# One-hot rows of a group by one VectorE comparison, and source lines of seven groups by one

## The chip, the cores and the metric

The program runs on one core of one Trainium2 chip. The metric is device time in microseconds (us) for one execution of the whole program, as the median of several runs. The engines are TensorE (PE, with its weight loads as PEld), VectorE (DVE), ScalarE (ACT), GpSimd (POOL) and SyncE (SP, which here only issues DMAs).

## What is computed

Four graph layers run one after the other on 3125 nodes of 32 features with 100000 edges sorted by destination. After each layer comes `x = layernorm(x + layer(x))`.

```
def _L0_gnn_ref(h, ...):                       # relation layer with attention
    x = h[src]; y = h[dst]
    msg = jnp.einsum('eb,ebo->eo', w_comp[etype], jnp.einsum('ei,bio->ebo', x, weight))
    a = tanh(relu(sum((x @ A1_w.T + A1_b) * (y @ A2_w.T + A2_b + rel_emb[etype]), -1) / scale))
    nei = segment_sum(a[:, None] * msg, dst)
    curr = h[src[last_e]] @ self_loop_weight   # last edge of each destination
    return relu(where(in_deg > 0, nei + curr, 0))
def _L1_gnn_ref(x, ...):  return segment_sum(x[src], dst)
def _L2_gnn_ref(h, ...):  softmax over a destination's edges, weighted sum of h[src]
def _L3_gnn_ref(feat, ...): ten steps of normalized propagation over the same edges
```

## The kernel before

There are two stages. The **sweep** (`run_sweep` on every engine) goes over the edges once. It computes layer 0 and, beside it, builds an adjacency matrix of edge counts, one byte for each pair of source and destination, in `adj_bytes`. The **dense** stage (`run_dense`) computes layers 1 to 3 as matrix products with that matrix. A general path for unsorted inputs exists and is not run.

The edges are cut into 196 groups of 512 (four slots of 128). For a group g the engines do this:

- **POOL** gathers the source rows of x by indirect DMA, one instruction for each 128 edges (line 587, 674 of them, into the ring `xp` of 21 groups). Of every seven groups one is *picked*: its rows come from TensorE products with one-hot matrices and POOL gathers nothing for it. POOL waits only until a ring place is free (`mixed_used`, g - 20), and starts with 21 groups ahead before the sweep.
- **SP** loads, for each *chunk* of seven groups, the relation and destination numbers of 3584 edges into 106 partitions (`load_lines`, two halves), and for every group the rows of the destination table; it also stores each group's result rows, one at a time (line 500).
- **DVE**, in this order for a group: `score_edges` (L1285, L1286), `make_pairs(g + 1)` (L1269, L1271), `make_line(g + 4)` (L1254), on some groups `make_dst_hot` (L1258), `make_pick_hots` (L1312: four compares on the second group of a chunk, three on the third) or `read_picked` (L1319, L1324), then `make_mixed` (L1293, L1296, L1300).
- **ACT**: the tanh of the scores (L1015), `make_rows(g + 2)` (L971, L975), the copy of the counts from PSUM (L980, L984), of the sums (L994), and the move of a page of counts into `adj_bytes` (L1008).
- **PE**: `fetch(g + 1)` (L696: destination and relation values by one-hot products with the compared lines), `count(g + 1)` (L709: adjacency counts, `row_hot` against `pair_hot`), on some groups `pick_tile` (L762), `sum_mixed(g)` (L728).

`row_hot` holds for each of the 512 edges a one-hot row of 128 over the low seven bits of its source; `pair_hot` a one-hot row over destination offset and the high bits. `row_no` and `pair_no` count columns; `row_f` and `pair_of` hold the wanted column of each edge, one value for each partition and slot. Before the change slot 0 of `row_hot` is made by ACT (`make_rows`: the square of the distance, then relu of one minus it), slots 1 to 3 by DVE, and `count` waits for both. `lines` holds two chunks; each group's 512 columns are compared in place with the partition's number (L1254), four groups ahead of use. The sweep's end passes through the last gather, the last group, its stores by SP, and a reload of the stored rows, for which the dense stage waits.

Of the kernel before, what the change touches and what calls it, by code (L numbers as in the profile page):

```python
# [21 lines left out]
P = 128  # L22
# [18 lines left out]
SLOTS = 4  # L41
GROUPS = -(-TILES // SLOTS)
# [18 lines left out]
LINE_AHEAD = 4  # L61
# [10 lines left out]
ROWS_BY_SCALAR = 1  # L72
# [88 lines left out]
def gnn(nc, x_pad, edges, src_cols, pick_rows, dst_cols, next_cols, bases, dst_rows_in, rel_rows_in, a1_rows, a2_rows, rel_emb_cols,  # L161
         weight, w_comp, w_comp_t, self_loop, a1_t, a2_t, rel_emb, attn_w, out):
    ctx = ExitStack()
    with ctx:
# [3 lines left out]
        def sem(name):  # L168
# [70 lines left out]
        row_f, pair_of, dst_off, last_off_1 = [stay.cut(GROUPS * SLOTS).rearrange("p (g k) -> p g k", k=SLOTS)  # L239
                                            for _ in range(4)]  # L240
# [142 lines left out]
        row_distances, row_hot_ready = sem("row_distances"), sem("row_hot_ready")  # L383
# [274 lines left out]
        def _(pe):  # L658
# [24 lines left out]
            def run_sweep():  # L683
                pe.wait_ge(sweep_cleared, 1)

                def fetch(g):
                    c = g // LINE
                    pe.wait_ge(lines_ready, g + 1)
                    pe.wait_ge(side_in[g % SIDES], 16 * (g // SIDES + 1))
                    if g >= 2:  # L690
                        pe.wait_ge(mixed_ready, g - 1)
                    for k in range(SLOTS):
                        at = FETCHED + g % 2 * BANK + k * REL_COLS
                        e = g % LINE * WINDOW + k * P
                        for j in range(3):
                            mm = nc.tensor.matmul(ps[:, at:at + REL_COLS], lines[:, c % 2, e:e + P], side[:, g % SIDES, j, :],  # L696
                                                  start=(j == 0), stop=(j == 2))
                    mm.then_inc(fetched, 1)

                def count(g):  # L700
                    pe.wait_ge(pairs_ready, g + 1)
                    pe.wait_ge(row_hot_ready, g + 1)
# [238 lines left out]
        def _(act):  # L941
# [21 lines left out]
            def run_sweep():  # L963
                act.wait_ge(sweep_cleared, 1)

                def make_rows(g):
                    h = g % 2
                    if g >= 2:
                        act.wait_ge(pairs_used, g - 1)
                    for k in range(ROWS_BY_SCALAR):  # L970
                        last = a.activation(row_hot[:, h, k, :], row_no[:], ACT.Square, bias=row_f[:, g, k:k + 1], scale=-1.0)  # L971
                    last.then_inc(row_distances, 1)
                    act.wait_ge(row_distances, g + 1)
                    hot_rows = row_hot[:, h, 0:ROWS_BY_SCALAR].rearrange("p k v -> p (k v)")
                    a.activation(hot_rows, hot_rows, ACT.Relu, bias=1.0, scale=-1.0).then_inc(row_hot_ready, 1)  # L975

# [34 lines left out]
                make_rows(0)  # L1011
                make_rows(1)
                for g in range(GROUPS):
# [3 lines left out]
                    if g + 2 < GROUPS:  # L1017
                        make_rows(g + 2)
# [100 lines left out]
        def _(dve):  # L1119
# [77 lines left out]
            link(v.tensor_copy(row_f, row_of))  # L1197
# [43 lines left out]
            def run_sweep():  # L1241
# [7 lines left out]
                def make_line(g):  # L1249
                    c = g // LINE  # L1250
                    if g % LINE == 0:
                        dve.wait_ge(line_in[c % 2], 32 * (c // 2 + 1))
                    own = lines[:, c % 2, g % LINE * WINDOW:(g % LINE + 1) * WINDOW]
                    v.tensor_scalar(own, own, side_no[0:SIDE, 1:2], None, ALU.is_equal).then_inc(lines_ready, 1)  # L1254
# [8 lines left out]
                def make_pairs(g):  # L1263
                    h = g % 2
                    if g >= 2:
                        dve.wait_ge(pairs_used, g - 1)
                    for k in range(SLOTS):
                        if k >= ROWS_BY_SCALAR:
                            v.tensor_scalar(row_hot[:, h, k, :], row_no[:], row_f[:, g, k:k + 1], None, ALU.is_equal)  # L1269
# [56 lines left out]

                for g in range(LINE_AHEAD):
                    make_line(g)
                make_dst_hot(0)
                make_pairs(0)  # L1330
                for g in range(GROUPS):
# [3 lines left out]
                    if g + LINE_AHEAD < GROUPS:  # L1335
                        make_line(g + LINE_AHEAD)
# [506 lines left out]
```

## Time and profile before

| | |
|---|---|
| median of 3 runs | 1260.72 us (1260.57 to 1262.55) |
| the profiled execution | 1265.35 us, its span 1263.6 us |
| sweep, about 57 to 930 us of the span | 196 groups |
| dense stage, from 934 us | TensorE at a granted clock of 0.95 |
| busy over the span | PE 77%, DVE 81%, ACT 50%, POOL 55% |
| from 190 to 890 us | DVE 85 to 90%, PE 74 to 81%, ACT 58 to 62%, POOL 77% |

An instruction's busy time is from its start to its end; instructions of one engine that do not wait for each other overlap by a part, so the distance of two starts is shorter than a duration. POOL's 77% is of the gather instructions alone: the time between them is told as idle, with its reason.

### The profile page before, as it was taken

The numbers are of one execution on the slowest core, as the hardware profiler recorded it, in microseconds if no ns is written. First come the engines' busy times: TensorE is split into PE (matmuls) and PEld (weight loads), VectorE is DVE, ScalarE is ACT, GpSimd is POOL, SyncE is SP. The second block draws the span as 40 slices with busy tenths as digits, with TensorE's granted clock in tenths as the row PEclk, the third lists the DMA queues.
The fourth block names the chain that finished last, engine by engine and source line by source line (L and its number), as shares of the span: only waits on it lengthen the run. The fifth ranks groups of instructions, "written<-read, shape, count | busy, mean of one in ns | idle before, by whom it ended". The sixth has DMA issues, their size and how long they took to land.

```text
span 1263.6 us, 58393 instructions
## 1 busy us (share of the span) xinstructions
PE 977.7 (77%) x23808; PEld 898.6 (71%) x23808; DVE 1020.9 (81%) x3443; ACT 638.0 (50%) x1731; POOL 698.4 (55%) x686
## 2 busy tenths in 40 slices
PE   2368788788788787787788677767827995999996
PEld 2357677677677676676677566666726995999996
DVE  8679999889888988898889888888844997655556
ACT  1146666656565555565566555555688980000000
POOL 5777777777777777777777777777600000000000
PEclk9557777777777767767777777767758997999998
DMA  4522222122222221122122212221100000000001
GB/s 108 73 46 56 51 46 46 46 48 48 47 46 46 46 45 45 45 46 45 45 46 46 44 46 45 45 45 41 18 14 3 3 4 3 4 4 4 4 4 18
DMA packets 55896, 46.32 MB, mean 37 GB/s; under 512 B 37442, under 2 KB 51837, under 8 KB 55624
## 3 DMA queue, kind: packets, MB, share of 16 engines
q1 hardware_dynamic: 34056, 31.45, 8.9%
q0 software_dynamic: 21568, 11.09, 6.9%
q8 instruction: 190, 3.11, 1.1%
q14 instruction: 82, 0.67, 0.2%
HBM read 40.19 MB, written 2.28 MB: 34 GB/s over the span
## 4 chain that ended last, share of the span: by engine, by line
PE 25%; DMA 21%; DVE 17%; issue 14%; SPq 11%; POOL 10%; ACT 1%; DVEq 0%; POOLq 0%; ACTq 0%
PE ps L820 12%; POOL arena L587 10%; DMA arena<-line_table 10%; DMA agg_table<-arena 8%; PE ps L762 3%; SPq L519 3%; SPq L496 3%; PE ps L728 3%; DMA arena<-x_pad,arena 3%; DVE arena L1271 2%; SPq L520 2%; SPq L500 2%; DVE arena L1465 2%; DVE arena L1269 1%; PE ps L709 1%
## 5 line engine op out<-in xcount | busy, mean ns | idle before, releaser
L587 POOL DMA_INDIRECT arena<-x_pad,arena x674 | 696.5, 1033 | 205.8 <-issue 200.3
L728 PE MATMUL ps<-arena 128*32 128x44 f32 (+3 forms) x7832 | 204.9, 234 | 152.5 <-DVE arena L1300 152.1
L728 PEld LDWEIGHTS ps<-arena 128*32 128x32 f32 x7832 | 152.4, 133 | 192.7 <-DVE arena L1300 167.3
L1271 DVE TENSOR_SCALAR arena<-pair_no,arena 128x275 bf16<-128x275 f16 (+2 forms) x784 | 239.2, 308 | 0.0
L820 PE MATMUL ps<-arena,adj_words 128*128 128x64 f16 (+1 forms) x6250 | 195.7, 193 | 24.5 <-DVEq L1415 21.8
L820 PEld LDWEIGHTS ps<-arena,adj_words 128*128 128x128 fp8e4 x6250 | 193.5, 98 | 26.6 <-DVEq L1415 22.6
L1300 DVE TENSOR_TENSOR arena<-ps,arena 128x768 f32<-128x768 f32 x196 | 188.0, 959 | 6.7
L709 PE MATMUL ps<-arena 128*128 128x175 bf16 (+3 forms) x1567 | 164.0, 261 | 31.3 <-DVE arena L1271 30.4
L762 PE MATMUL ps<-aggT 128*128 128x128 bf16 x2268 | 175.3, 244 | 0.0
L1015 ACT ACTIVATE arena<-arena 128x4 f32<-128x4 f32 x196 | 40.2, 205 | 266.7 <-DVE arena L1286 255.9
L762 PEld LDWEIGHTS ps<-aggT 128*128 128x128 bf16 x2268 | 159.2, 112 | 0.0
L1269 DVE TENSOR_SCALAR arena<-row_no,arena 128x128 bf16<-128x128 bf16 x588 | 159.1, 272 | 0.0
L1008 ACT ACTIVATE adj_words<-arena 128x500 uint8 x196 | 126.2, 644 | 49.4 <-issue 38.6
L709 PEld LDWEIGHTS ps<-arena 128*128 128x128 bf16 x1567 | 121.0, 115 | 37.1 <-DVE arena L1271 36.1
L696 PE MATMUL ps<-arena 106*128 106x49 bf16 x2352 | 112.1, 201 | 7.7 <-DMA arena<-dst_parts 7.7
L984 ACT ACTIVATE arena<-ps 128x500 fp8e4<-128x500 f32 x196 | 113.2, 577 | 0.0
L980 ACT ACTIVATE arena<-ps 128x500 bf16<-128x500 f32 x196 | 111.6, 569 | 0.0
L1089 ACT ACTIVATE stat<-stat,eps 128x4 f32<-128x4 f32 (+3 forms) x9 | 2.7, 299 | 214.7 <-DVEq L1376 214.7
L1254 DVE TENSOR_SCALAR arena<-arena,side_no 106x512 bf16<-106x512 bf16 x196 | 67.2, 344 | 48.4 <-DMA arena<-line_table 48.4
L696 PEld LDWEIGHTS ps<-arena 106*128 106x128 bf16 x2352 | 93.5, 108 | 10.6 <-issue 7.9
L1285 DVE TENSOR_TENSOR arena<-ps,arena 128x132 f32<-128x132 f32 x196 | 56.3, 287 | 35.8 <-DMA arena<-x_pad,arena 24.8
L971 ACT ACTIVATE arena<-row_no,arena 128x128 bf16<-128x128 bf16 x196 | 75.7, 386 | 10.6 <-DVEq L1247 10.5
(213 smaller groups left out, 1261.7 us busy)
## 6 DMA issues: line engine op xcount, KB each, us to landing
arena<-line_table SPq DMA_DIRECT2D x28, 602.0 KB
arena<-x_pad,arena POOLq DMA_INDIRECT x674, 3.3
arena<-line_table SPq DMA_DIRECT2D x28, 140.0 KB
arena<-pick_table SPq DMA_DIRECT2D x27, 128.0 KB
arena<-dst_parts SPq DMA_DIRECT2D x196, 5.7 KB
agg_table<-arena SPq DMA_DIRECT2D x196, 2.5 KB
dst_parts<-aggT SPq DMA_DIRECT2D x1, 735.0 KB, 14.7
x<-x_pad SPq DMA_DIRECT2D x1, 400.0 KB
```

The lines of the kernel that those rows point to most:

```text
L587: pool.indirect_dma_start(to, None, table, bass.IndirectOffsetOnAxis(ap=index, axis=0)).then_inc(done, 16)
L696: mm = nc.tensor.matmul(ps[:, at:at + REL_COLS], lines[:, c % 2, e:e + P], side[:, g % SIDES, j, :], start=(j == 0), stop=(j == 2))
L709: mm = nc.tensor.matmul(ps[:, at + d0 * BLOCKS:at + d1 * BLOCKS], row_hot[:, h, k, :], pair_hot[:, h, k, (d0 - first) * BLOCKS:(d1 - first ...
L728: return nc.tensor.matmul(to.rearrange("p (d m) -> p d m", m=MIX_COLS)[:, :, 0:m1 - m0], rows_of_slot, factors[:, :, m0:m1], start=False, ...
L762: mm = nc.tensor.matmul(ps[:, at:at + PICK_WIDE * FEAT], pick_hot[:, j, k * P:(k + 1) * P], x_parts[:, t, j * PICK_WIDE:(j + 1) * PICK_WID ...
L820: mm = nc.tensor.matmul(ps[:, at:at + cols], adj[:, b, j * P:(j + 1) * P], parts[:, half, b, 0:cols], start=(b == 0), stop=(b == BLOCKS - 1))
L980: a.activation(squares, ps[:, at:at + PAIRS], ACT.Square, accum_out=square_sums[:, g:g + 1])\
L984: a.activation(pages[:, g % PAGES], ps[:, at:at + PAIRS].rearrange("p (d b) -> p b d", d=PAGE), ACT.Copy, saturate=False).then_inc(counts_ ...
L1008: a.activation(adj_bytes[:, :, bass.ds(base, PAGE)], page_bytes[:, g % PAGES], ACT.Copy)\
L1269: v.tensor_scalar(row_hot[:, h, k, :], row_no[:], row_f[:, g, k:k + 1], None, ALU.is_equal)
L1271: last = v.tensor_scalar(pair_hot[:, h, k, 0:n], pair_no[:, 0:n], pair_of[:, g, k:k + 1], None, ALU.is_equal)
L1300: v.tensor_tensor(mixed[:, g % 2, :, :, 0:BASES], fetched_of(g)[:, :, SCORED:REL_COLS].unsqueeze(2).to_broadcast(n), weighted.unsqueeze(3) ...
```

## The change

Three things are changed, all in the sweep.

1. **Rows.** A new table `row_twice` replaces `row_f`: the wanted column of each edge as a two-byte number, written twice side by side (one copy of 1568 elements before the sweep, where 784 were copied). `make_pairs` then makes all four slots of `row_hot` with one tensor_tensor compare of 512 elements for each partition, and after it the four compares of `pair_hot`, now back to back. `make_rows` and its two ACT instructions for each group are gone, with their semaphores, and `count` waits for DVE alone.
2. **Lines.** One tensor_scalar compare covers the 3584 columns of a chunk, where there were seven of 512.
3. **Their place.** The first chunk is compared before the loop, and chunk c + 1 in group 5 of chunk c (`LINES_AT`), after the pair compares. TensorE's `fetch` waits once for each chunk.

```
@@ -69,7 +68,7 @@
-ROWS_BY_SCALAR = 1
+LINES_AT = LINE - 2
@@ -236,8 +235,8 @@
-        row_f, pair_of, dst_off, last_off_1 = [stay.cut(GROUPS * SLOTS)...
+        pair_of, dst_off, last_off_1 = [stay.cut(GROUPS * SLOTS)... for _ in range(3)]
+        row_twice = stay.cut(2 * GROUPS * SLOTS, BF16).rearrange("p (g k i) -> p g k i", k=SLOTS, i=2)
@@ -685,7 +683,8 @@ (fetch)
-                    pe.wait_ge(lines_ready, g + 1)
+                    if g % LINE == 0:
+                        pe.wait_ge(lines_ready, c + 1)
@@ -699,7 +698,6 @@ (count)
-                    pe.wait_ge(row_hot_ready, g + 1)
@@ -1008,14 +995,10 @@ (ACT)
-                    if g + 2 < GROUPS:
-                        make_rows(g + 2)
@@ -1194,7 +1177,7 @@
-            link(v.tensor_copy(row_f, row_of))
+            link(v.tensor_copy(row_twice, row_of.unsqueeze(3).to_broadcast([P, GROUPS, SLOTS, 2])))
@@ -1246,11 +1229,9 @@
-                def make_line(g):
...
-                    own = lines[:, c % 2, g % LINE * WINDOW:(g % LINE + 1) * WINDOW]
+                def make_lines(c):
+                    dve.wait_ge(line_in[c % 2], 32 * (c // 2 + 1))
+                    own = lines[:, c % 2, :]
                     v.tensor_scalar(own, own, side_no[0:SIDE, 1:2], None, ALU.is_equal).then_inc(lines_ready, 1)
@@ -1264,9 +1245,11 @@ (make_pairs)
+                    n = [P, SLOTS, P // 2, 2]
+                    v.tensor_tensor(row_hot[:, h].rearrange("p k (v i) -> p k v i", i=2),
+                                    row_no[:].rearrange("p (v i) -> p v i", i=2).unsqueeze(1).to_broadcast(n),
+                                    row_twice[:, g].unsqueeze(2).to_broadcast(n), ALU.is_equal)
                     for k in range(SLOTS):
-                        if k >= ROWS_BY_SCALAR:
-                            v.tensor_scalar(row_hot[:, h, k, :], row_no[:], row_f[:, g, k:k + 1], None, ALU.is_equal)
                         n = PAIR_DSTS[k] * BLOCKS
                         last = v.tensor_scalar(pair_hot[:, h, k, 0:n], ...
@@ -1324,16 +1307,15 @@ (the loop over groups)
-                    if g + LINE_AHEAD < GROUPS:
-                        make_line(g + LINE_AHEAD)
+                    if g % LINE == LINES_AT and g // LINE + 1 < LINES:
+                        make_lines(g // LINE + 1)
```

On DVE, the second group of the first chunk stands like this before (from its score to the four pick compares):

```order
L1285 TENSOR_TENSOR arena<-ps,arena 128x132
L1286 TENSOR_REDUCE arena<-arena 128x4
L1271 TENSOR_SCALAR arena<-pair_no,arena 128x200
L1269 TENSOR_SCALAR arena<-row_no,arena 128x128
L1271 TENSOR_SCALAR arena<-pair_no,arena 128x275
L1269 TENSOR_SCALAR arena<-row_no,arena 128x128
L1271 TENSOR_SCALAR arena<-pair_no,arena 128x275
L1269 TENSOR_SCALAR arena<-row_no,arena 128x128
L1271 TENSOR_SCALAR arena<-pair_no,arena 128x300
L1254 TENSOR_SCALAR arena<-arena,side_no 106x512
L1312 TENSOR_SCALAR aggT<-arena,pick_no 128x512 x4
```

and now (numbers of the changed file: L1268 and L1269 are the score, L1249 the rows, L1254 the pairs, L1295 the picks):

```order
L1268 TENSOR_TENSOR arena<-ps,arena 128x132
L1269 TENSOR_REDUCE arena<-arena 128x4
L1249 TENSOR_TENSOR arena<-row_no,arena 128x512
L1254 TENSOR_SCALAR arena<-pair_no,arena 128x200
L1254 TENSOR_SCALAR arena<-pair_no,arena 128x275 x2
L1254 TENSOR_SCALAR arena<-pair_no,arena 128x300
L1295 TENSOR_SCALAR aggT<-arena,pick_no 128x512 x4
```

The three row compares and the line compare in front of the picks are gone, and the rows stand ahead of the pairs as one instruction. The line compare now stands in the sixth group of the chunk, behind the pairs (L1235 is the line compare):

```order
L1249 TENSOR_TENSOR arena<-row_no,arena 128x512
L1254 TENSOR_SCALAR arena<-pair_no,arena 128x200
L1254 TENSOR_SCALAR arena<-pair_no,arena 128x275 x2
L1254 TENSOR_SCALAR arena<-pair_no,arena 128x300
L1235 TENSOR_SCALAR arena<-arena,side_no 106x3584
L1276 TENSOR_TENSOR arena<-next_no,arena 128x48
```

It is seven times as wide as the one that stood in every group. POOL's, PE's and SP's instructions stay what they are and in their order.

## Rows read from the trace of the kernel before

**Rows 1.** Source view of POOL's gathers: ns min/median/max, then who ended waits.

```profile
L587 POOL DMA_INDIRECT arena<-x_pad,arena x674: 941/947/2317, 11.3 to 912.1; - x169
  issue: 200.3, 656
  PE ps L728: 5.5, 18
```

**Rows 2.** The page's group of the gathers: busy us, mean ns | idle before.

```profile
L587 POOL DMA_INDIRECT arena<-x_pad,arena x674 | 696.5, 1033 | 205.8 <-issue 200.3
```

**Rows 3.** Busy time in three stretches of the sweep, columns as headed.

```profile
core 0: us, PE busy (x) PEld busy (x) DVE busy (x) ACT busy (x) POOL busy (x), PEclk, DMA share, GB/s
190.00:290.00 100.00, 80.62 (x1759) 71.79 (x1759) 89.96 (x335) 60.83 (x190) 77.36 (x75) 0.74 0.20 46
790.00:890.00 100.00, 74.68 (x1655) 66.02 (x1654) 84.70 (x313) 57.93 (x181) 77.12 (x76) 0.73 0.20 42
```

**Rows 4.** Timeline of a group with picks: start us, us, instruction [idle before].

```profile
215.01 0.25 DVE L1269 TENSOR_SCALAR arena<-row_no,arena 128x128 bf16<-128x128 bf16 x1
215.09 2.18 POOL L587 DMA_INDIRECT arena<-x_pad,arena  x1 [0.30 <-issue]
215.18 0.29 DVE L1271 TENSOR_SCALAR arena<-pair_no,arena 128x275 bf16<-128x275 f16 x1
...
215.75 0.35 DVE L1254 TENSOR_SCALAR arena<-arena,side_no 106x512 bf16<-106x512 bf16 x1
216.01 1.14 DVE L1312 TENSOR_SCALAR aggT<-arena,pick_no 128x512 bf16<-128x512 f16 x4
```

**Rows 5.** The gathers from 306.5 to 313 us, beside a chunk's two pick bursts.

```profile
L587 POOL DMA_INDIRECT arena<-x_pad,arena x5 | 6.2, 1243 | 1.5 <-issue 1.5
```

**Rows 6.** The gathers from 374.5 to 398 us, with no pick burst.

```profile
L587 POOL DMA_INDIRECT arena<-x_pad,arena x20 | 19.1, 956 | 6.1 <-issue 6.1
```

**Rows 7.** DVE's groups by form: busy us, mean ns | idle before, releaser.

```profile
L1300 DVE TENSOR_TENSOR arena<-ps,arena 128x768 f32<-128x768 f32 x196 | 188.0, 959 | 6.7
...
L1254 DVE TENSOR_SCALAR arena<-arena,side_no 106x512 bf16<-106x512 bf16 x196 | 67.2, 344 | 48.4 <-DMA arena<-line_table 48.4
...
L1312 DVE TENSOR_SCALAR aggT<-arena,pick_no 128x512 bf16<-128x512 f16 x189 | 53.9, 343 | 0.0
...
L1258 DVE TENSOR_TENSOR arena<-hot_no,arena 128x336 bf16<-128x336 bf16 x28 | 13.9, 497 | 0.0
```

**Rows 8.** Timeline: a copy of 2058 columns, and four line compares, beside gathers.

```profile
47.26 0.75 DVE L1224 COPY arena<-arena 86x2058 bf16<-86x2058 bf16 x1
47.28 0.94 POOL L587 DMA_INDIRECT arena<-x_pad,arena  x1 [0.30 <-issue]
...
57.05 1.29 DVE L1254 TENSOR_SCALAR arena<-arena,side_no 106x512 bf16<-106x512 bf16 x4 [2.81 <-DMA arena<-line_table]
57.28 0.95 POOL L587 DMA_INDIRECT arena<-x_pad,arena  x1 [0.31 <-issue]
```

**Rows 9.** Timeline: two tensor_tensor instructions with both inputs in SBUF, beside gathers.

```profile
21.57 0.98 DVE L1177 TENSOR_TENSOR arena<-arena 128x784 f32<-128x784 int32 x1
21.65 1.71 POOL L587 DMA_INDIRECT arena<-x_pad,arena  x1 [0.30 <-issue]
...
318.49 0.49 DVE L1258 TENSOR_TENSOR arena<-hot_no,arena 128x336 bf16<-128x336 bf16 x1
318.75 1.04 POOL L587 DMA_INDIRECT arena<-x_pad,arena  x1 [0.31 <-issue]
```

**Rows 10.** SP's line loads of two chunks, from its own timeline.

```profile
302.73 0.24 SPq L478 DMA_DIRECT2D arena<-line_table  x1
...
332.52 0.24 SPq L478 DMA_DIRECT2D arena<-line_table  x1
```

**Rows 11.** The sweep's end: the last gather, and the dense stage's first DVE instruction.

```profile
912.08 0.94 POOL L587 DMA_INDIRECT arena<-x_pad,arena  x1 [0.30 <-issue]
...
933.74 0.08 DVE L1402 MEMSET arena<- 128x25 f16 x1 [10.97 <-DMA agg<-agg_table]
```

More of the change, by code:

```diff
@@ L60 @@
 STORE_DELAY = SIDES + 10
-LINE_AHEAD = 4
 LINE_ROWS = 98
@@ L238, in gnn @@
         base_t = stay.cut(GROUPS + 1, I32)
-        row_f, pair_of, dst_off, last_off_1 = [stay.cut(GROUPS * SLOTS).rearrange("p (g k) -> p g k", k=SLOTS)
-                                            for _ in range(4)]
+        pair_of, dst_off, last_off_1 = [stay.cut(GROUPS * SLOTS).rearrange("p (g k) -> p g k", k=SLOTS) for _ in range(3)]
+        row_twice = stay.cut(2 * GROUPS * SLOTS, BF16).rearrange("p (g k i) -> p g k i", k=SLOTS, i=2)
         xp = stay.cut(AHEAD * SLOTS * SCORED).rearrange("p (u k c) -> p u k c", u=AHEAD, k=SLOTS)
@@ L382, in gnn @@
         lines_ready, fetched = sem("lines_ready"), sem("fetched")
-        row_distances, row_hot_ready = sem("row_distances"), sem("row_hot_ready")
         pairs_ready, pairs_used = sem("pairs_ready"), sem("pairs_used")
@@ L964, in run_sweep @@
                 act.wait_ge(sweep_cleared, 1)
[L966 to L975, printed above, removed]
                 def copy_counts(g):
@@ L1009, in move_page @@
                      .then_inc(pages_moved, 1)
-                make_rows(0)
-                make_rows(1)
                 for g in range(GROUPS):
@@ L1247, in run_sweep @@
                 dve.sem_inc(sweep_cleared, 1)
-                def make_line(g):
-                    c = g // LINE
-                    if g % LINE == 0:
-                        dve.wait_ge(line_in[c % 2], 32 * (c // 2 + 1))
-                    own = lines[:, c % 2, g % LINE * WINDOW:(g % LINE + 1) * WINDOW]
+                def make_lines(c):
+                    dve.wait_ge(line_in[c % 2], 32 * (c // 2 + 1))
+                    own = lines[:, c % 2, :]
                     v.tensor_scalar(own, own, side_no[0:SIDE, 1:2], None, ALU.is_equal).then_inc(lines_ready, 1)
@@ L1325, in read_picked @@
                                          picked.rearrange("p (k w f) -> p k f w", k=SLOTS, w=PICK_WIDE), AX.X, ALU.add))
-                for g in range(LINE_AHEAD):
-                    make_line(g)
+                make_lines(0)
                 make_dst_hot(0)
```

## The prediction

> **What bounds the kernel now.** The page's busy shares point at DVE (85 to 90% in the sweep), and the change takes work from it. I read POOL first all the same, since 77% is a strange number for an engine with one kind of instruction. The stretches show that it does not move: 77.36 us of 100 early, 77.12 late, 75 and 76 gathers, while DVE falls from 90 to 85 [rows 3]. The source view tells why. A gather takes 947 ns in the median, and almost all of POOL's idle time, 200.3 us, is "issue", that is, no one was waited for; the only named releaser, TensorE, has 18 gaps with 5.5 us together, 0.3 us each, the same gap as any other [rows 1]. So POOL issues gathers back to back from 11.3 to 912.1 us, with 0.30 us between them [rows 1, 4]. Its ring lets it run 21 groups ahead, it never waits for a free place, and so nothing that DVE gains can start a gather earlier.
>
> The account closes: 674 x (0.947 + 0.305) = 844 us, plus the start at 11.3, is 855 us; the last gather starts at 912.1 and ends at 913.0 [rows 1, 11]. The missing 58 us are gathers that took longer: their mean is 1033 ns, and 674 x (1033 - 947) ns = 58 us [rows 2]. **The sweep's length is this floor plus the stretch of the gathers.** Behind the last gather come the last group, its stores and the reload, until the dense stage starts at 933.74 [rows 11]; these follow the gather and are not changed.
>
> What stretches a gather is seen beside DVE. Where four pick compares of 1.14 us run, the gather under them takes 2.18 us [rows 4]. The five gathers around one chunk's two bursts have a mean of 1243 ns, 5 x 0.296 = 1.48 us over the floor [rows 5]; twenty gathers without a burst 956 ns, 0.2 us over it in all [rows 6]. With 27 chunks that have picks the bursts hold 27 x 1.48 = 40 us of the 58, and 18 us lie elsewhere.
>
> So the question is not what DVE saves but what the new instructions do to the gathers.
>
> **The change part by part.** The sum is made against the profiled execution of 1265.35 us (span 1263.6, 1.75 around it) and moved to the median, 1260.72, which lies 4.63 lower.
>
> *DVE and ACT time saved.* A row compare starts 0.17 us before the next instruction (215.01 to 215.18) [rows 4], so three cost 0.5 us for each group; one tensor_tensor of 512 takes their place. For that one the trace has bounds: 343 ns, the one-input compare of 512 two-byte columns, below; above, the slope of the tensor_tensor rows, (959 - 497) / (768 - 336) = 1.07 ns a column, gives 497 + 176 x 1.07 = 685 ns [rows 7]. I take the middle, about 0.5 us: the rows alone save DVE nothing much, between +0.2 and -0.2 us a group. Of the lines, seven that start 0.26 us before the next (215.75 to 216.01) [rows 4] make 1.8 us; the wide one is worked out from the copy of 2058 columns in 0.75 us [rows 8] and the 344 ns of 512 [rows 7]: (751 - 344) / 1546 = 0.26 ns a column, so 0.75 + 1526 x 0.26 ns = 1.15 us. That is 0.7 us a chunk. The 48.4 us that DVE waits for line loads [rows 7] go too, as the compare stands two groups later against its load. All this is costed at nothing: POOL's stream covers it. ACT's two instructions are beside the stream as well, and TensorE's waits for lines and rows are met at least as early as before (the lines a group ahead of need, the rows ahead of the pairs); the change adds no wait to any queue. If that cover were gone, DVE's gain would show; that is a rival below.
>
> The Trainium skill (VectorE: DVE Perf Modes, "The perf-mode tier table") lets a tensor_tensor of two-byte operands run at two columns a cycle. The tensor_tensor rows here run at one; by the page the new instruction would take some 0.42 us, an estimate from that page, and no number of the sum would change.
>
> *The wide line compare, 27 in the stream.* It stands in a group without picks and behind four pair compares. The burst rows price DVE compares of this kind: 1.48 us of stretch [rows 5] for one burst of 1.14 us [rows 4] and one of three compares, some 0.87 us, so 0.74 us for each us; 1.15 us would cost 0.85. Against it stand two rows: four line compares in a row, 1.29 us, beside a gather of 0.95 us, and a copy of 0.75 us from just before a gather of 0.94 us [rows 8], no stretch. The bounds are 0 and 0.85 us each, 0 to 23 us. I take nearer the burst, which is the same kind of long unbroken work in the same stage, while the other rows are from one moment each: 0.55, so **+15 us**.
>
> *The 196 small line compares taken away.* One stood directly ahead of every burst and made it 0.26 us longer [rows 4]: 54 bursts x 0.26 x 0.74 = 10 us. Elsewhere they share the 18 us that are not the bursts'; I give them 4. So **-14 us**, bounds -18 and -4.
>
> *The row compare with two inputs in SBUF, 196.* The rows that show such an instruction by itself both show a stretch: 0.98 us makes a gather of 1.71, and L1258's 0.49 us one of 1.04, 0.09 over the floor [rows 9]. Short ones do nothing that shows: L1293, also with two inputs in SBUF, runs in each group of rows 6, where the mean is 956. The bounds are 0 and 0.09 each, 0 to 18 us; half, **+9 us**. The row compares that go were in the chain with the pairs and cost next to nothing: all of the chains are within the 0.2 us of rows 6.
>
> The Trainium skill (SBUF — State Buffer, "Who interferes with whom") says that VectorE and GpSimd share one pair of ports as an exclusive lock, that a tensor_tensor takes only its read side, and infers that making descriptors for a gather needs the write side, so that tensor_tensor does not hold a gather up. The 1.71 us of rows 9 speak against that inference. By the page the third term would be zero and the sum +1, one more way to the third rival.
>
> *Before the sweep* a copy of 1568 elements replaces one of 784, some 0.4 us of DVE; POOL gathers its first 21 groups meanwhile and does not wait for it.
>
> Sum: 15 - 14 + 9 = **+10 us**: 1275.4 for a profiled execution, 1270.7 as a median.
>
> **The rivals.**
>
> 1. *The wide compare holds no gather* (as in rows 8). Then -14 and a smaller third term of +3: -11, 1250 us. For it: the four line compares in a row. Against it: each burst of picks that I looked at stretched a gather.
> 2. *Pair compares back to back act like a burst.* Before, a row compare stood between each two. Four in a row last some 0.8 us; at half the burst's price 196 x 0.3 = 59 us: 1320 us. For it: the bursts are just such runs of one kind. Against it: four line compares in a row did no harm, and pairs and rows are as unbroken today. It decides against me from 0.05 us a group on.
> 3. *The terms cancel* (or the tensor_tensor costs nothing): within 2.5 us of 1260.7.
> 4. *DVE is the bound after all*, and its freed time comes off the end. The next limit would be SP's loop, whose chunks are 332.52 - 302.73 = 29.8 us apart [rows 10], against POOL's 24 x (1.033 + 0.305) = 32.1 [rows 1, 2]: 27 x 2.3 = 62 us off, 1199 us. For it: the 85 to 90% [rows 3]. Against it: POOL's gaps, which name no one [rows 1].
>
> **How the numbers follow.** Forecast (slower by 3 to 35 us) 0.52; rival 1 0.20; rival 2 0.08; rival 3 0.15; rival 4 0.05. A measurement tells 0.2%, 2.5 us, from no change. So faster 0.20 + 0.05 = 0.25, same 0.15, slower 0.52 + 0.08 = 0.60. The bounds of the terms are 0 - 18 + 0 = -18 and 23 - 4 + 18 = +37. The range leaves out rivals 2 and 4 and the outermost corner of the terms where all three lie at their ends: 1248 to 1298. The forecast's own range is 1263 to 1296.
>
> **What would show each step right or wrong.** POOL's stream must again be without waits, with 0.30 us between gathers and a median of 947 ns; if its gaps name TensorE, or the median moves, the frame is wrong. Its mean tells the sum: 1033 + 10000 / 674 = 1048 ns by the forecast, 1017 by the first rival, 1120 by the second. Gathers beside the wide compare should be 1.5 us in the mean if 0.55 is right, and 0.95 if it holds none. Gathers around a chunk's picks should have a smaller mean than 1243 ns. DVE should lose its 48.4 us of waits for lines and wait for gathers in their place, from early in the sweep. The dense stage should keep its length. What would make it wrong without any of this: that the gathers and DVE's groups fall into a fixed step, since DVE would then wait for a landing in most groups, and each of the small costs would be paid always or never.

## The result, and the profile after

The changed kernel takes 1249.41 us in the median of four runs (1246.71 to 1253.19) against 1260.99 for the kernel before: a ratio of 0.9908, 95% interval 0.9883 to 0.9933. It is 0.9% faster; slower by 0.8% was forecast. The profiled execution is the fastest of the four, 1246.71 us with a span of 1244.9, 18.7 less than the 1263.6 of before. The medians lie only 11.6 us apart: the profiled execution of before, 1265.35 us, is 4.4 us above its median, that of after 2.7 below. The account that follows is of these two executions.

The frame of the prediction first. The source view of POOL's gathers (ns min/median/max, first and last start, then what ended the waits) and the page's group of them (busy us, mean ns | idle before):

```profile
L585 POOL DMA_INDIRECT arena<-x_pad,arena x674: 940/945/1889, 11.1 to 880.8; - x169
  issue: 202.0, 662
  PE ps L726: 3.7, 12
```

```profile
L585 POOL DMA_INDIRECT arena<-x_pad,arena x674 | 665.5, 987 | 205.6 <-issue 202.0
```

Against [rows 1, 2] the median (945 ns for 947), the gaps and their reason are the same; POOL still never waits. Only the mean fell, 1033 to 987 ns, and the longest gather from 2317 to 1889 ns. Summed over the 674 gathers, the stretch (what a gather takes beyond 947 ns) fell from 58.2 to 27.3 us, and the last gather starts 31 us earlier, 880.8 for 912.1 [rows 11].

Where the 31 us went is seen beside DVE. A group with four picks, as in [rows 4], from the timeline (start us, us, instruction, [idle before]):

```profile
200.34 0.87 DVE L1254 TENSOR_SCALAR arena<-pair_no,arena 128x200 bf16<-128x200 f16 x4
200.48 0.95 POOL L585 DMA_INDIRECT arena<-x_pad,arena  x1 [0.30 <-issue]
201.13 1.19 DVE L1295 TENSOR_SCALAR aggT<-arena,pick_no 128x512 bf16<-128x512 f16 x4
...
201.73 0.94 POOL L585 DMA_INDIRECT arena<-x_pad,arena  x1 [0.30 <-issue]
```

The same four picks that stood beside a gather of 2.18 us now stand beside one of 0.94. The five gathers from 200.9 to 206.5 us, around both bursts of a chunk, have a mean of 968 ns where [rows 5] had 1243:

```profile
L585 POOL DMA_INDIRECT arena<-x_pad,arena x5 | 4.8, 968 | 1.5 <-issue 1.5
```

The wide line compare costs what was forecast. Its group (busy us, mean ns | idle before, releaser) with that of the new row compare, then one of them beside a gather:

```profile
L1249 DVE TENSOR_TENSOR arena<-row_no,arena 128x512 bf16<-128x512 bf16 x196 | 82.0, 418 | 0.0
...
L1235 DVE TENSOR_SCALAR arena<-arena,side_no 106x3584 bf16<-106x3584 bf16 x28 | 32.9, 1173 | 76.5 <-DMA arena<-line_table 76.5
```

```profile
216.90 1.61 POOL L585 DMA_INDIRECT arena<-x_pad,arena  x1 [0.31 <-issue]
...
217.25 1.15 DVE L1235 TENSOR_SCALAR arena<-arena,side_no 106x3584 bf16<-106x3584 bf16 x1
```

Each gather's stretch, put down to what DVE ran beside it (worked out from the records of both kernels, in us over the sweep; a gather beside several of these is put down to the first in the table):

| beside | before | after |
|---|---|---|
| pick compares | 42.9 | 3.5 |
| small line compares, away from picks | 8.8 | |
| wide line compare | | 16.1 |
| row compares | 0.2 | 0.4 |
| destination one-hots (L1258, now L1239) | 1.4 | 0.5 |
| other, and ahead of the sweep | 4.9 | 6.8 |
| sum | 58.2 | 27.3 |

Before, 185 gathers stood beside row compares and beside none of the others; they have 0.1 us in all.

But the span gained 18.7 us, not 31. The end of the sweep, from POOL's, SP's and DVE's timelines:

```profile
880.79 0.94 POOL L585 DMA_INDIRECT arena<-x_pad,arena  x1 [0.30 <-issue]
```

```profile
873.34 35.62 SPq L498 DMA_DIRECT2D agg_table<-arena  x25
909.85 0.43 SPq L525 DMA_DIRECT2D agg<-agg_table  x1
```

```profile
914.39 0.08 DVE L1384 MEMSET arena<- 128x25 f16 x1 [22.91 <-DMA agg<-agg_table]
```

The dense stage starts 32.7 us behind the last gather, where it was 20.7 [rows 11]. SP issues 25 stores one behind the other, each waiting some 1.4 us for the one before, and the reload follows the last. DVE waits 22.91 us for it, where it waited 10.97. SP got there late because its loop is slow: in the list of waits of SP's queue (us in total, times, longest) a store waits up to 11.4 us for the store before it, which stands behind the line load in the same queue; with the loads in another queue (below, loads by ACT) the same waits are 86.9 us in all, 4.5 at worst:

```profile
SPq L497 <- DMA agg_table<-arena: 263.0, 32, 11.4
```

DVE, too, waits more for line loads than before, 76.5 us against 48.4 [rows 7]. From 914.39 on nothing changed: 330.5 us to the end of the span, 329.8 before.

### The profile page after: what moved, and what is told of

It reads as the page before. It is cut to its first block, busy times and chain, and to the rows that moved or that the text cites. A ratio compares the mean times of both kernels' runs of the same rounds, so it can differ in the third digit from the quotient of the medians.

```text
span 1244.9 us, 57245 instructions
## 1 busy us (share of the span) xinstructions
PE 961.3 (77%) x23808; PEld 887.5 (71%) x23808; DVE 967.4 (78%) x2883; ACT 527.9 (42%) x1339; POOL 667.4 (54%) x686
## 4 chain that ended last, share of the span: by engine, by line
DMA 29%; PE 20%; SPq 19%; DVE 17%; issue 15%; ACT 1%; DVEq 0%; POOLq 0%; ACTq 0%; POOL 0%
DMA agg_table<-arena 15%; PE ps L818 13%; DMA arena<-line_table 12%; SPq L517 5%; SPq L494 5%; SPq L518 3%; SPq L498 3%; DVE arena L1254 2%; DVE arena L1447 2%; PE ps L726 1%; DVE arena L1283 1%; DVE arena L1235 1%; DVE arena L1467 1%; PE ps L789 1%; PE ps L760 1%
## 5 line engine op out<-in xcount | busy, mean ns | idle before, releaser
L585 POOL DMA_INDIRECT arena<-x_pad,arena x674 | 665.5, 987 | 205.6 <-issue 202.0
L726 PE MATMUL ps<-arena 128*32 128x44 f32 (+3 forms) x7832 | 200.8, 231 | 159.8 <-DVE arena L1283 159.7
L726 PEld LDWEIGHTS ps<-arena 128*32 128x32 f32 x7832 | 148.9, 130 | 199.9 <-DVE arena L1283 175.0
L818 PE MATMUL ps<-arena,adj_words 128*128 128x64 f16 (+1 forms) x6250 | 195.6, 193 | 37.2 <-DVEq L1397 33.8
L1254 DVE TENSOR_SCALAR arena<-pair_no,arena 128x275 bf16<-128x275 f16 (+2 forms) x784 | 177.9, 295 | 0.0
L707 PE MATMUL ps<-arena 128*128 128x175 bf16 (+3 forms) x1567 | 158.7, 255 | 10.3 <-DVE arena L1254 9.4
L1235 DVE TENSOR_SCALAR arena<-arena,side_no 106x3584 bf16<-106x3584 bf16 x28 | 32.9, 1173 | 76.5 <-DMA arena<-line_table 76.5
L1249 DVE TENSOR_TENSOR arena<-row_no,arena 128x512 bf16<-128x512 bf16 x196 | 82.0, 418 | 0.0
L1545 DVE TENSOR_REDUCE work<-ps 128x128 f32<-128x256 f32 (+1 forms) x70 | 27.7, 396 | 65.9 <-PE ps L818 57.2
L981 ACT COPY arena<-ps 128x100 f32<-128x100 f32 x196 | 48.0, 245 | 67.4 <-PE ps L726 52.9
```

Source lines behind the costliest of these rows:

```text
L585: pool.indirect_dma_start(to, None, table, bass.IndirectOffsetOnAxis(ap=index, axis=0)).then_inc(done, 16)
L707: mm = nc.tensor.matmul(ps[:, at + d0 * BLOCKS:at + d1 * BLOCKS], row_hot[:, h, k, :], pair_hot[:, h, k, (d0 - first) * BLOCKS:(d1 - first ...
L726: return nc.tensor.matmul(to.rearrange("p (d m) -> p d m", m=MIX_COLS)[:, :, 0:m1 - m0], rows_of_slot, factors[:, :, m0:m1], start=False, ...
L818: mm = nc.tensor.matmul(ps[:, at:at + cols], adj[:, b, j * P:(j + 1) * P], parts[:, half, b, 0:cols], start=(b == 0), stop=(b == BLOCKS - 1))
L1249: v.tensor_tensor(row_hot[:, h].rearrange("p k (v i) -> p k v i", i=2), row_no[:].rearrange("p (v i) -> p v i", i=2).unsqueeze(1).to_broad ...
L1254: last = v.tensor_scalar(pair_hot[:, h, k, 0:n], pair_no[:, 0:n], pair_of[:, g, k:k + 1], None, ALU.is_equal)
```

## The experiments

A burst is the row of three or four pick compares of a group; there are 54. "Stretch at picks" is the sum of what the gathers beside bursts take beyond 947 ns; a burst counts as held if the gathers beside it are over 250 ns longer in all. "Behind" is from the end of the last gather to the first dense instruction on DVE. Ratios are to the kernel before, on the same chip.

| kernel | ratio (95% interval) | mean gather ns | stretch at picks us | bursts held | last gather ends | dense starts | behind |
|---|---|---|---|---|---|---|---|
| before | 1 | 1033 | 42.9 | 54 | 913.0 | 933.7 | 20.7 |
| after | 0.9908 (0.9883 to 0.9933) | 987 | 3.5 | 1 | 881.7 | 914.4 | 32.7 |
| rows alone | 0.9964 (0.9950 to 0.9978) | 1015 | 33.8 | 54 | 900.7 | 918.4 | 17.7 |
| lines alone | 0.9912 (0.9896 to 0.9929) | 990 | 5.7 | 5 | 883.7 | 916.0 | 32.3 |
| before, line behind picks | 0.9973 (0.9962 to 0.9984) | 975 | 5.7 | 3 | 873.5 | 924.8 | 51.3 |
| after, seven line compares | 0.9890 (0.9874 to 0.9907) | 968 | 4.5 | 4 | 868.7 | 910.1 | 41.4 |
| after, compare of 106 ahead | one run: 1279.42 us | 1056 | 37.6 | 54 | 928.8 | 946.6 | 17.8 |
| after, compare of 128 ahead | one run: 1244.23 us | 988 | 2.5 | 1 | 881.9 | 913.1 | 31.2 |
| before, lines on 128 | 0.9978 (0.9963 to 0.9992) | 992 | 16.8 | 14 | 885.3 | 933.5 | 48.2 |
| after, lines on 128 | 0.9885 (0.9870 to 0.9900) | 989 | 4.8 | 4 | 883.3 | 920.5 | 37.2 |
| before, loads by ACT | 1.0005 (0.9988 to 1.0021) | 1031 | 41.6 | 54 | 911.0 | 930.6 | 19.6 |
| after, loads by ACT | 0.9776 (0.9751 to 0.9800) | 988 | 3.2 | 5 | 882.4 | 901.5 | 19.1 |
| after, loads by ACT, seven | 0.9696 (0.9674 to 0.9719) | 974 | 2.7 | 2 | 872.9 | 890.5 | 17.6 |
| the same, lines on 128 | 0.9666 (0.9650 to 0.9682) | 971 | 3.5 | 2 | 871.4 | 889.1 | 17.7 |

### Which part freed the picks

Two theories stood after the result: T1, that the small line compare ahead of a burst had held the gathers; T2, that the row compares of before had. Each part was made alone.

*Rows alone*: the changed kernel with a small line compare for each group, where it stood before (shown: the place in the loop).

```
-                    if g % LINE == LINES_AT and g // LINE + 1 < LINES:
-                        make_lines(g // LINE + 1)
+                    if g + LINE_AHEAD < GROUPS:
+                        make_line(g + LINE_AHEAD)
```

> The rows part of the change alone: one two-byte compare for row_hot, none by ScalarE, but the line compares as before, one of 512 columns in each group, directly ahead of the picks. In the changed kernel the gathers are stretched by 27 us over 674 x 947 ns (16 us of it beside the wide line compare, 3.5 beside the picks), before by 58 us (43 beside the picks). Theory 1: it is the line compare directly ahead of a pick burst that makes the burst hold the gathers. Then the picks' 43 us come back, the wide compare's 16 go: mean gather about 1022 ns, and the time about 1257 us. Theory 2: it is the single-input row compares in the chain ahead of the picks. Then the picks stay cheap: mean gather about 964 ns, time 1240 to 1250 us.

*Lines alone*: the kernel before, its row compares and ACT's among them, with the wide line compare (the same lines the other way round).

> The lines part alone: one compare of 3584 columns for each chunk in its sixth group; rows as before, slot 0 by ScalarE and three small compares between the pairs. Theory 1 (line ahead of the picks): the picks hold no gather any more, the wide compare costs its 16 us: mean gather about 987 ns, time near the changed kernel's 1249 us. Theory 2 (row compares ahead of the picks): the picks keep their 43 us and the wide compare adds 16: mean gather about 1050 ns, time about 1270 us.

*Before, line behind picks*: the kernel before with nothing changed but the place of its small line compare.

```
-                    if g + LINE_AHEAD < GROUPS:
-                        make_line(g + LINE_AHEAD)
...
+                    if g + LINE_AHEAD < GROUPS:
+                        make_line(g + LINE_AHEAD)
```

> The kernel before with one thing moved: the small line compare of each group stands behind the picks (and what reads picked rows) instead of ahead of them. Same instructions. Theory 1: picks hold no gather, so about 40 us of stretch go: mean gather about 975 ns, last gather at about 873 us; the time falls by less, since SP's stores then end the sweep, to about 1245 to 1250 us. Theory 2: nothing changes, mean 1033 ns, 1260 us.

With the line compare ahead, all 54 bursts hold their gathers, whichever row compares stand there (42.9 and 33.8 us); without it five and three do (5.7 us in both). The page's gather groups of the three kernels, in that order:

```profile
L585 POOL DMA_INDIRECT arena<-x_pad,arena x674 | 684.2, 1015 | 205.7 <-issue 198.7
```

```profile
L587 POOL DMA_INDIRECT arena<-x_pad,arena x674 | 667.4, 990 | 205.7 <-issue 202.7
```

```profile
L587 POOL DMA_INDIRECT arena<-x_pad,arena x674 | 657.3, 975 | 205.7 <-issue 201.1
```

T1 holds, and T2 falls as the cause at the bursts. T1's own sizes for the first two kernels, 1022 and about 987 ns, were near (1015 and 990). The third shows that neither the number of compares in a row nor their columns hold a gather: the same instructions stand there, with the line compare last.

The time did not follow. The third kernel's gathers end at 873.5 as T1 said, 39.5 us earlier than before, and yet it takes 1254.68 us in the median where T1 had 1245 to 1250.

### What in the line compare holds them

Two changed kernels with one compare added ahead of each burst, its result never read; they differ in the number of partitions alone.

```
+        more = sb('more', [P, WINDOW], BF16)
...
+                    j = blocks[0]
+                    v.tensor_scalar(more[0:SIDE, :], codes[0:SIDE, c % 2, :], pick_no[0:SIDE, j:j + 1], None, ALU.is_equal)
                     for j in blocks:
```

(SIDE is 106.) In the second, `[0:SIDE]` is `[:]`, that is 128.

> The changed kernel with one more VectorE compare ahead of each burst of pick compares: 106 partitions x 512, two-byte, the shape of the small line compare, its result never read. Theory A (any 512-column compare at that place holds the gathers): the gathers beside pick bursts stretch by 34 to 43 us in all, as in the kernel before (42.9) and with its line compare put back (33.8); mean of a gather 1035 to 1050 ns. Theory B (it was the line compare itself, its operands or its semaphore, and not a compare at that place): under 8 us, mean 985 to 1000 ns. The end of the span follows: by A the last gather ends near 915 us and the span is 1262 to 1268 us, by B 882 us and 1245 to 1252 us.

> The same with 128 partitions: the first pick compare of each burst is made twice, once into a tile that nobody reads, so that five (four) equal ones stand in a row. Theory A: as above, 34 to 43 us of stretch, mean 1035 to 1050 ns. Theory B: under 8 us, mean 985 to 1000 ns. If this one holds the gathers and the 106-partition one does not, it is the length of the row of equal operations.

Timeline of one burst with 106 partitions, then with 128; L1296 is the added compare, L1298 the picks:

```profile
150.66 0.43 DVE L1296 TENSOR_SCALAR more<-arena,pick_no 106x512 bf16<-106x512 f16 x1
151.01 1.12 DVE L1298 TENSOR_SCALAR aggT<-arena,pick_no 128x512 bf16<-128x512 f16 x4
151.28 1.91 POOL L586 DMA_INDIRECT arena<-x_pad,arena  x1 [0.30 <-issue]
```

```profile
151.46 0.41 DVE L1296 TENSOR_SCALAR more<-arena,pick_no 128x512 bf16<-128x512 f16 x1
151.79 1.33 DVE L1298 TENSOR_SCALAR aggT<-arena,pick_no 128x512 bf16<-128x512 f16 x4
152.06 0.94 POOL L586 DMA_INDIRECT arena<-x_pad,arena  x1 [0.30 <-issue]
```

Both gathers start 0.27 us into the picks. Behind 106 partitions DVE runs through (1.12 us) and the gather takes 1.91; behind 128 the gather takes 0.94 and DVE gives way (1.33 us). All 54 bursts against one: 37.6 us of stretch against 2.5. How the gathers happen to lie to the bursts is not the reason: with the last gather begun about 0.98 us ahead of the first pick, all eight bursts of the one kernel hold and none of the twenty of the other, and at about 0.39 us all four against none of 19. So neither theory was put rightly: it is not any compare at that place, and not the line compare's data or semaphore either, but one on 106 partitions ahead of ones on 128. Other numbers of partitions were not tried, and why the number matters no run here shows.

The kernel with 106 partitions is slower than theory A had it, a span of 1277.6 us for 1262 to 1268. Besides the bursts, the 28 destination one-hots (L1240 there) hold gathers: 24 gathers begun 0.04 us into one took 1.27 us each, 7.8 us in all, where the changed kernel has 0.5.

The kernel before was then given lines of 128 partitions, 22 of them read by nobody.

```
-        lines = sweep.cut(2 * LINE * WINDOW, BF16, n=SIDE)...
+        lines = sweep.cut(2 * LINE * WINDOW, BF16)...
+            link(v.memset(arena[96:P, stay.at:stay.at + NODES_PAD], 0.0))
-                    v.tensor_scalar(own, own, side_no[0:SIDE, 1:2], None, ALU.is_equal)...
+                    v.tensor_scalar(own, own, side_no[:, 1:2], None, ALU.is_equal)...
```

(TensorE still reads 106.)

> The kernel before with its small line compare made on all 128 partitions instead of 106 (22 rows that nobody reads; a memset of 2.7 us ahead of the sweep makes them defined). Theory H (an operation on fewer than 128 partitions ahead of full ones is what holds the gathers): stretch beside pick bursts falls from 42.9 us to under 8, mean of a gather 975 to 990 ns, last gather 873 to 885 us; SyncE then ends the sweep, and the span is 1244 to 1256 us. If the line compare holds them for another reason (its operands, its semaphore): 35 us or more of stretch, the span as before, 1260 to 1266 us.

40 of the 54 bursts let the gathers through, 14 still hold them, 16.8 us where under 8 was expected. Those 14 lie close together in how far ahead of the first pick the last gather had started: 0.72, 0.93 to 0.95 or 1.04 to 1.08 us; in the kernel before it holds at all the distances that occur, 0.18 to 1.25 us. All 14 gathers were in flight when the burst began; no gather that began inside a burst is held any more, where before 20 were. Held bursts of the other kernels cluster too (the four of the kernel with seven line compares are all at 0.30 to 0.31 us). So with 106 partitions a hold that comes at some distances came in every burst. Why at those is open. The span, 1263.8 us, did not fall to the 1244 to 1256 that theory H had; what kept it is shown below.

### What the wide compare costs, and why

*After, seven line compares*: the 3584 columns as seven compares of 512, one behind the other.

```
-                    own = lines[:, c % 2, :]
-                    v.tensor_scalar(own, own, side_no[0:SIDE, 1:2], None, ALU.is_equal).then_inc(lines_ready, 1)
+                    for n in range(LINE):
+                        own = lines[:, c % 2, n * WINDOW:(n + 1) * WINDOW]
+                        last = v.tensor_scalar(own, own, side_no[0:SIDE, 1:2], None, ALU.is_equal)
+                    last.then_inc(lines_ready, 1)
```

> The changed kernel with the wide line compare cut into seven of 512 columns, back to back in the same place. If it is the long single instruction that holds the gathers, the 16 us beside it go: mean gather about 964 ns, last gather at about 866 us. If it is DVE's busy time of about 2 us in a row, they stay: 987 ns or more. By both the time moves little, within 3 us of 1249, if SP's stores are what ends the sweep; if the gathers still set the end, the first gives 1233 us.

*After, lines on 128*: the wide compare on 128 partitions, with the edit shown above.

> The changed kernel with its wide line compare (3584 columns) on 128 partitions instead of 106. If the number of partitions is also what makes the wide compare hold a gather: its 16.1 us of stretch fall under 5, the last gather ends at 866 to 871 us, and the time falls by 3 to 6 us as in the seven-compare kernel, SyncE ending the sweep. If it is the length of one operation: 14 to 18 us of stretch as before, gathers end at 880 to 884 us, the time is the changed kernel's within 3 us.

Cut into seven, the compares hold no gather to speak of (0.4 us over the sweep where the wide one cost 16.1):

```profile
308.17 2.07 DVE L1236 TENSOR_SCALAR arena<-arena,side_no 106x512 bf16<-106x512 bf16 x7 [2.83 <-DMA arena<-line_table]
308.37 0.97 POOL L585 DMA_INDIRECT arena<-x_pad,arena  x1 [0.30 <-issue]
309.64 0.94 POOL L585 DMA_INDIRECT arena<-x_pad,arena  x1 [0.30 <-issue]
```

On 128 partitions the wide one costs the same, 16.2 us:

```profile
342.33 1.70 POOL L585 DMA_INDIRECT arena<-x_pad,arena  x1 [0.30 <-issue]
342.76 1.16 DVE L1236 TENSOR_SCALAR arena<-arena,side_no 128x3584 bf16<-128x3584 bf16 x1 [1.91 <-DMA arena<-line_table]
```

Here it is the length of one instruction. In both kernels with the wide compare the gathers it holds end at fixed distances behind it, 0.12 us (12 of 28 in each) or 0.8 us (16), whatever their start: it too is a hold until the end. The gathers of the seven-compare kernel end 13 us earlier than after's, and the span gains 4.1: again the end did not follow.

### What ends the sweep

The line loads of chunks 1 to 27 were given to ACT's queue, so that no store stands behind them in SP's; the rest is as it was.

```
-                        if c >= 2:
-                            sp.wait_ge(fetched, (c - 1) * LINE)
-                        if c >= 1:
-                            load_lines(c)
...
+                    if g % LINE == 0 and g // LINE + 1 < LINES:
+                        load_by_act(g // LINE + 1)
```

(The lines taken out are SP's, the new ones stand in ACT's loop; `load_by_act` makes the same wait and issues the same two loads by ACT, at the head of the chunk before.) On the changed kernel:

> The changed kernel with the line loads of chunks 1 to 27 issued from ScalarE's queue instead of SyncE's, so that no row store waits behind them. Theory S (in the changed kernel SyncE's stores end the sweep, not the gathers): gathers as in the changed kernel (mean 987 ns, last one at 882 us), the dense part starts 18 to 21 us behind the last gather instead of 32.7, at 900 to 903 us, and the span is 331 us more: 1231 to 1234 us, 12 to 14 less than the changed kernel. Theory G (the gathers still set the end): no change, 1245 to 1249 us. Theory D (VectorE or TensorE are next): between, with VectorE waits on TensorE in place of those on line loads.

With the seven compares as well:

> The same with the wide line compare cut into seven of 512 columns back to back. By theory S the gathers end at 866 to 870 us as in the seven-compare kernel, the dense part starts 18 to 21 us later and the span is 1216 to 1222 us; the 16 us that the wide compare cost the gathers now count in full, where they counted 4 us in the measured span when SyncE ended the sweep. By theory G or D it stays at 1230 us or more.

On the kernel before:

> The kernel before with the line loads of chunks 1 to 27 issued from ScalarE's queue. If the prediction's frame held for the kernel before (the gathers set the end of the sweep there, SyncE only followed), nothing moves: gathers as before (mean 1033 ns, last one at 913 us), the dense part starts at 930 to 934 us, time within 4 us of before. If SyncE's stores already set the end in the kernel before, it is 8 us or more faster.

And the second one with lines on 128 partitions:

> Line loads by ScalarE's queue and seven line compares in a row (the fastest so far), the compares on 128 partitions. By theory H the four rows of seven that held a gather for 1.4 us each (6.9 us in all) go, the last gather ends at 866 to 869 us and the span is 1214 to 1220 us; otherwise as that kernel, 1220 to 1224 us.

The last gather and the dense start of the kernel with loads by ACT and seven compares:

```profile
871.95 0.94 POOL L581 DMA_INDIRECT arena<-x_pad,arena  x1 [0.30 <-issue]
```

```profile
890.47 0.08 DVE L1396 MEMSET arena<- 128x25 f16 x1 [8.43 <-DMA agg<-agg_table]
```

Theory S holds. The dense stage is again 17.6 to 19.1 us behind the last gather; the changed kernel gains 11.6 us of span (1244.9 to 1233.3) with gathers that did not move. Only with the loads on ACT's queue is it worth something to cut the wide compare: 11.2 us of span (1233.3 to 1222.1), against 4.1 without. The kernel before does not move at all (1.0005): there the gathers did set the end, as the prediction had it. But SP was right behind. With lines on 128 partitions its gathers end at 885.3, 27.7 us earlier, and the dense stage starts at 933.5, where it started before:

```profile
884.40 0.94 POOL L587 DMA_INDIRECT arena<-x_pad,arena  x1 [0.30 <-issue]
```

```profile
888.83 39.32 SPq L500 DMA_DIRECT2D agg_table<-arena  x25
929.04 0.43 SPq L527 DMA_DIRECT2D agg<-agg_table  x1
```

The last kernel, 1223.12 us in the median (1219.68 to 1225.02), and the one with the compares on 106 partitions, 1222.46 (1219.99 to 1224.96), hardly differ; their ratios, 0.9666 and 0.9696, have intervals that just overlap. On 128 partitions one row of the 28 held a gather where four had, and 6.9 us of stretch beside the seven line compares became 2.1; but the last gather ends at 871.4, not at 866 to 869 as theory H had it, so these runs do not decide about the 106 partitions there. Both beat the two kernels of this case, by 3% the one before the change.

What stays open is SP's own pace. Its line loads, from the first chunk's to the last, are 30.2 us apart before, 30.1 with the line behind the picks and 30.3 with lines on 128, but 29.8 after and in the rows alone, 29.7 in the lines alone. Over 27 chunks that is up to 16 us in the SP-bound kernels' ends, and no run here separates its cause.

## Why the prediction was wrong

**The frame held, for the kernel before.** POOL issues without waits, the median stayed (945 ns for 947), and the sum of stretches tells where the last gather ends. Loads by ACT on the kernel before (ratio 1.0005) shows that SP's stores did not set the end there.

**The wide line compare, +15 us: measured 16.1.** That is 0.57 us for each of 28 (one of them ahead of the loop), nearer to the burst than to the single moments of [rows 8], as chosen. Gathers beside it took 1.25 to 1.89 us, or 1.41 to 1.66 behind one of 0.95. That the size came out is in part luck: it was priced like a burst, as long unbroken work, but seven compares of the same columns, 2.07 us unbroken, cost 0.4 us in all, and what holds the gathers at a burst is the compare ahead of it. The first rival, that it holds no gather, is false, although its 1250 us is the time that came out.

**The small line compares, -14 us: measured -37 at the bursts alone** (42.9 to 5.7 in the lines alone), and -8.8 elsewhere, where it had -4. This is the step that failed. The prediction took the stretch at a burst to be the picks' own, in proportion to their duration, 0.74 us for each us, and gave the compare ahead of them only its own 0.26 us: 10 us of 40. The rows could not tell the picks from the compare ahead, since [rows 4] shows the one never without the other, and [rows 6] has groups without picks, so the line compare without picks, and no stretch. That pair of rows says that both are needed or that the picks do it; the prediction read only the second. The records of before held one more hint. The gathers in flight when a burst of four began ended 0.12 us after its last compare, whatever their start: begun 0.33, 0.54, 0.71 and 0.92 us ahead of the picks they were 0.63, 0.84, 1.02 and 1.23 us over the floor. The 20 that began inside a burst ended 0.81 to 1.06 us after it. That is a hold until the end, and a price for each us of DVE work does not describe one.

**The row compare with two inputs, +9 us: measured 2.7.** Its 418 ns is below the 0.5 us taken. From the page of the Trainium skill (VectorE: DVE Perf Modes, "The perf-mode tier table") the prediction had estimated 0.42 us, and the trace agrees. 190 gathers ran beside it and beside no pick or line compare, with 0.4 us of stretch in all; the 156 of them in flight when it began took 0.95 us at most. But a gather that begins inside it waits. Each of the 29 gathers begun 0.05 to 0.28 us into a row compare (22 of them stood beside picks or a line compare too and are counted there in the table) ended 0.81 to 0.82 us after it, one of them here:

```profile
516.93 0.42 DVE L1249 TENSOR_TENSOR arena<-row_no,arena 128x512 bf16<-128x512 bf16 x1
517.01 1.16 POOL L585 DMA_INDIRECT arena<-x_pad,arena  x1 [0.31 <-issue]
```

Both gathers of [rows 9] end 0.81 us after their instruction as well, and so do, at 0.82, the 24 beside the destination one-hots of the kernel with the compare of 106 ahead. So [rows 9] were read rightly as a stretch, but its size depends on where the gather begins and on how long the instruction still runs, and 418 ns leave little: 2.7 us for the 29. The Trainium skill (SBUF — State Buffer, "Who interferes with whom") infers that a tensor_tensor does not hold up a gather's descriptors; the 156 in flight agree, the 29 begun inside do not.

**"These follow the gather and are not changed": wrong by 12 us.** SP's stores came last, 32.7 us behind the last gather for 20.7. The prediction did name SP as next in its fourth rival, with 29.8 us for each chunk (one chunk's distance; the mean of that kernel is 30.2), and put that limit 62 us away. It left out what comes behind the loop: the stores run 24 groups late, and 25 of them take 35.6 us. The room was not 62 us; with lines on 128 partitions the kernel before shows next to none.

**DVE's 48.4 us of waits for lines should have gone: they grew to 76.5.** DVE was no longer held back by gathers and met SP's pace. With loads by ACT, one such wait of 2.8 us is left, and DVE waits for gathers instead, 69.2 us, as was forecast for the changed kernel.

Together, by the table of stretches: 16.1 - 39.4 - 8.8 + 0.2 - 0.9 + 1.9 = -30.9 us for the gathers where +10 was forecast, and +12 for the stores behind them, -19 us, against -18.7 in the span of the two profiled executions (-11.6 in the medians). Of the rivals, the second (pair compares back to back act like a burst) did not come: the 84 gathers beside pair compares and none of the instructions of that table have 2.2 us of stretch in the whole sweep. The range of 1248 to 1298 us was not quite what the prediction says of it: its upper end is the outermost corner of the terms, +37, which it says is left out. The change is mostly its second part: lines alone give 0.9912, rows alone 0.9964.

## What to carry to other kernels

When an engine's operations are now and then twice as long, line up their ends with the other engine's work: an end that is the same whatever the start is a hold, and its cause is to be sought at what stands at its beginning. Before an account of the bounding engine is turned into time, work out when the next engine in line would end by itself, its drain behind the loop included; a change that frees the first is worth no more than that distance. A small transfer that waits for its predecessor does not belong in a queue with large loads.

## What was not expected of the hardware

- A two-byte tensor_scalar of 512 columns on 106 partitions, directly ahead of ones on 128, held a gather until the last of the row had ended, in 54 of 54 bursts (37.6 us): 32 gathers in flight, which ended 0.12 us after the row or a little before, and 22 begun inside it, which ended 0.81 to 1.06 us after it. The same on 128 partitions did it in one of 54 (2.5 us). With a 106-partition one behind them, in the kernel before, it was three of 54.
- The hold goes beyond one instruction. The Trainium skill (SBUF — State Buffer, "Who interferes with whom") says that whoever issues first has the ports that VectorE and GpSimd share for the whole instruction, and the other blocks. Both directions are seen here: picks of 1.12 us beside a gather of 1.91, and of 1.33 beside one of 0.94. But the 1.91 us reach over the row of four, not over one instruction of 0.34 us.
- Seven compares of 512 columns on 106 partitions, 1.97 to 2.36 us without a gap, let gathers of 0.94 to 1.06 us through in all 28 rows; one of 3584 columns and 1.15 us made them 1.25 to 1.89. In the kernel with loads by ACT, four such rows of 28 held a gather all the same, 1.4 us each, all with the gather begun 0.26 to 0.35 us ahead of the first of the seven.
- A two-input instruction held the gathers that began inside it and not those in flight: behind row compares of 418 ns, 29 of 29 begun 0.05 to 0.28 us into one ended 0.81 to 0.82 us after it, while 156 in flight took 0.95 us at most.
